# Attention's prologue in a four-stage image kernel: key copies issued from ScalarE's queue, and the first phase's row maxima taken over both PSUM banks at once

## What is computed

```python
qkv = einsum('oc,bct->bot', qkv_w, xf) + qkv_b            # 256 -> 768, t = 1024
scores = einsum('bthe,bThe->bhtT', q, k) / sqrt(32)
attn = softmax(scores, axis=-1)
out = einsum('bhtT,bThe->bthe', attn, v)
```

## Time and profile before

| | us |
|---|---|
| median of 3 runs | 5492.75 (5491.58 to 5498.53) |
| the profiled execution, its own time | 5495.14 |
| its span | 5493.3 |
| granted TensorE clock, mean | 0.853 |
| PE / DVE / ACT / POOL busy | 77% / 66% / 39% / 37% |
| 16 attentions, each with a prologue of some 38 us from the first head to the transposed maxima | about 610 |

### The profile page before, as it was taken

The page is one execution under the profiler, slowest core; times in us unless marked ns, Lnnn a source line. Parts: engine busy times, 40 slices in busy tenths (PEclk is TensorE's granted clock), DMA queues, the critical chain, the costliest instruction groups (busy, mean ns, idle before and its releaser), DMA issues.

```text
span 5493.3 us, 44457 instructions
## 1 busy us (share of the span) xinstructions
PE 4249.1 (77%) x16298; PEld 1843.1 (34%) x16298; DVE 3607.0 (66%) x4793; ACT 2146.6 (39%) x2639; POOL 2007.6 (37%) x681
## 2 busy tenths in 40 slices
PE   5688866879668896688866878669796697866978
PEld 2243422434224332243322433224332243322333
DVE  6763677637776368764687646867468674686746
ACT  3233452334423354243542425424254242542524
POOL 3531435404344043440444504434044340443404
PEclk7689977999769997799977999779897798977999
DMA  0020100210002100022000120011200112001020
GB/s 36 0 55 19 29 8 7 48 29 19 8 8 47 34 14 8 9 47 44 3 8 14 41 46 1 8 25 30 46 1 8 31 24 46 1 8 29 19 46 9
DMA packets 62956, 125.75 MB, mean 23 GB/s; under 512 B 18825, under 2 KB 21001, under 8 KB 62482
## 3 DMA queue, kind: packets, MB, share of 16 engines
q1 hardware_dynamic: 62738, 122.91, 9.6%
HBM read 12.23 MB, written 8.39 MB: 4 GB/s over the span
## 4 chain that ended last, share of the span: by engine, by line
PE 47%; DVE 28%; issue 10%; ACT 7%; SPq 4%; POOL 2%; DMA 2%; DVEq 0%; ACTq 0%; POOLq 0%
DVE mx L954 9%; PE PS L1250 8%; PE PS L1292 8%; PE PS L1087 7%; PE PS L1340 7%; PE PS L1374 4%; DVE work L846 3%; DVE work L848 3%; PE PS L1146 3%; PE PS L1184 2%; ACT PT L624 2%; SPq L290 2%; PE PS L1301 2%; SPq L299 2%; POOL work L392 1%
## 5 line engine op out<-in xcount | busy, mean ns | idle before, releaser
L954 DVE TENSOR_REDUCE mx<-PS 128x1 f32<-128x512 f32 x2048 | 1338.1, 687 | 422.0 <-PE PS L1250 417.9
L624 ACT ACTIVATE PT<-PS 128x1024 f32<-128x1024 f32 x1024 | 1006.9, 1023 | 689.9 <-PE PS L1340 660.0
L1250 PE MATMUL PS<-KS,QS 96*128 96x512 f32 x2048 | 894.9, 479 | 195.4 <-DMA KS<-piece 84.7
L408 POOL TENSOR_TENSOR piece<-PT 128x2048 f32<-128x2048 f32 x48 | 220.0, 4584 | 2183.4 <-ACT PT L624 2183.4
L408 POOL TENSOR_TENSOR piece<-piece,PT 128x2048 f32<-128x2048 f32 x192 | 878.0, 4573 | 58.4 <-ACT PT L624 47.1
L388 POOL TENSOR_TENSOR work<-work,Crep 128x1024 f32<-128x1024 f32 x256 | 616.3, 2409 | 390.5 <-DVE work L846 193.1
L1340 PE MATMUL PS<-QS,KS 98*128 98x512 f32 x2048 | 681.4, 424 | 45.9 <-DMA QS<-nm 22.2
L1250 PEld LDWEIGHTS PS<-KS,QS 96*128 96x128 f32 x2048 | 378.0, 197 | 816.2 <-DVE mx L954 578.0
L1292 PE MATMUL PS<-PT,Vt 128*32 128x512 f32 x4096 | 546.0, 605 | 27.0 <-ACT PT L624 27.0
L1184 PE MATMUL PS<-dstk,sel 128*128 128x512 f32 (+1 forms) x640 | 315.7, 568 | 321.1 <-DVE work L848 133.0
L542 ACT ACTIVATE PS<-PS,Aneg 128x1024 f32<-128x1024 f32 x256 | 278.3, 1087 | 628.5 <-PE PS L1184 597.8
(11 more groups left out here) (198 smaller groups left out, 4983.0 us busy)
## 6 DMA issues: line engine op xcount, KB each, us to landing
QS<-piece SPq DMA_DIRECT2D x384, 128.0 KB, 2.4
KS<-piece SPq DMA_DIRECT2D x384, 128.0 KB, 2.4
xin<-x SPq DMA_DIRECT2D x8, 1024.0 KB
out<-xr SPq DMA_DIRECT2D x8, 1024.0 KB, 4.0
W<-wpack SPq DMA_DIRECT2D x2, 1024.0 KB
QS<-nm SPq DMA_DIRECT2D x128, 8.0 KB, 1.9
W<-wpack SPq DMA_DIRECT2D x1, 576.0 KB
W<-wpack SPq DMA_DIRECT2D x2, 256.0 KB
```

What stands on the lines that cost most here:

```text
L408: pool.tensor_tensor(total, first, PT[:, i % 3, :, :], ALU.add).then_inc(sum_pool.sem, 1)
L624: act.activation(PT[:, i % 3, 2 * pr:2 * pr + 2, :], PS[:, 2 + 2 * pr:4 + 2 * pr, :], ACT.Exp, scale=SCALE).then_inc(p_sb.sem, 1)
L954: dve.tensor_reduce(mx[:, at, cc:cc + 1], PS[:, row_slot(n, cc), :], AX.X, ALU.max).then_inc(r_max.sem, 1)
L1250: pe.matmul(PS[:, row_slot(n, cc), :], QS[0:kd, c, h, q * P:q * P + P], KS[0:kd, h, cc * N:cc * N + N], start=True, stop=True).then_inc(r_ ...
```

## The change

Three edits, all in the prologue of the 16 attentions:

1. The 12 key copies of a group are issued by ScalarE instead of SP, after ScalarE has written both heads of the group and waited for the keys' rest. SP issues the 12 query copies in one go.
2. In phase 0 a row's maximum is one reduction over both halves (1024 scores, two banks), straight into `mboth`. It releases both halves at once (`r_max` rises by two). The joining reduction L961 is gone in phase 0, as is its semaphore step: the transpose waits for the last row's `r_max`.
3. The semaphore `m_both` counts one phase less, and the joining reduction waits in every phase where it is left for the transpose before it.

```diff
@@ sync engine
                     sp.wait_ge(*qk_rest(b, n + 1))
-                    for j in range(AHEAD):
+                    for j in range(GH):
                         queries(j)
-                    sp.wait_ge(*qk_rest(b, n + 2))
-                    for j in range(GH):
-                        for blk, part in enumerate((0, 0, 1)):
-                            sp.dma_start(KS[...], piece[32 * j:32 * j + 32, 1, part, :]).then_inc(stackedk[g][j].sem, 16)
-                        if j + AHEAD < GH:
-                            queries(j + AHEAD)
@@ ScalarE, attention, behind both heads of a group
+                    act.wait_ge(*qk_rest(b, 4 * a + 2 * g + 2))
+                    for j in range(GH):
+                        for blk, part in enumerate((0, 0, 1)):
+                            act.dma_start(KS[...], piece[32 * j:32 * j + 32, 1, part, :]).then_inc(stackedk[g][j].sem, 16)
@@ VectorE, phase 0
                 for n in range(PHASE_ROWS):
-                    for cc in range(NC):
-                        row_max(n, cc)
+                    dve.wait_ge(*r_ps(b, halves(a, n, NC - 1) + 1))
+                    dve.tensor_reduce(mboth[:, n:n + 1], PS[:, row_slot(n, 0):row_slot(n, 0) + NC, :].rearrange("p a n -> p (a n)"),
+                                      AX.X, ALU.max).then_inc(r_max.sem, NC)
@@ TensorE, turn_max
-                    pe.wait_ge(*m_both(b, a * PHASES + ph + 1))
+                    if ph == 0:
+                        pe.wait_ge(*r_max(b, halves(a, PHASE_ROWS - 1, NC - 1) + 1))
+                    else:
+                        pe.wait_ge(*m_both(b, a * (PHASES - 1) + ph))
```

More of the change, by code:

```diff
@@ L53 @@
 TURN_AT = 7
-AHEAD = 3
 NORM_AT = 4
@@ L241, in build @@
         r_ps, r_max = sig("r_ps", 2 * HEADS * KT * NC), sig("r_max", 2 * HEADS * KT * NC)
-        m_both = sig("m_both", 2 * PHASES)
+        m_both = sig("m_both", 2 * (PHASES - 1))
         mt_ps, nm_head, nm_rest = (sig(n, 2 * PHASES) for n in ("mt_ps", "nm_head", "nm_rest"))
@@ L293, in attention @@
                     sp.wait_ge(*qk_rest(b, n + 1))
-                    for j in range(AHEAD):
+                    for j in range(GH):
                         queries(j)
-                    sp.wait_ge(*qk_rest(b, n + 2))
-                    for j in range(GH):
-                        for blk, part in enumerate((0, 0, 1)):
-                            sp.dma_start(KS[32 * blk:32 * blk + 32, GH * g + j, :].bitcast(F32),
-                                         piece[32 * j:32 * j + 32, 1, part, :].bitcast(F32)).then_inc(stackedk[g][j].sem, 16)
-                        if j + AHEAD < GH:
-                            queries(j + AHEAD)
                 for ph in range(PHASES):
@@ L589, in attention @@
                                        bias=v(bq, 2 * kind + g)).then_inc(qk_head.sem, 1)
+                    act.wait_ge(*qk_rest(b, 4 * a + 2 * g + 2))
+                    for j in range(GH):
+                        for blk, part in enumerate((0, 0, 1)):
+                            act.dma_start(KS[32 * blk:32 * blk + 32, GH * g + j, :].bitcast(F32),
+                                          piece[32 * j:32 * j + 32, 1, part, :].bitcast(F32)).then_inc(stackedk[g][j].sem, 16)
                 for q in range(2):
@@ L958, in row_max @@
                         dve.wait_ge(*r_max(b, halves(a, n, NC - 1) + 1))
-                        if ph > 0:
-                            dve.wait_ge(*mt_ps(b, PHASES * a + ph))
+                        dve.wait_ge(*mt_ps(b, PHASES * a + ph))
                         dve.tensor_reduce(mboth[:, :], mx[:, :, :], AX.X, ALU.max).then_inc(m_both.sem, 1)
```

## The result

| | before | with the change |
|---|---|---|
| median of 17 executions each, us | 5493.05 (5489.31 to 5499.03) | 5506.96 (5500.40 to 5518.02) |
| ratio of the times | | 1.0024, 95% interval 1.0017 to 1.0031 |
| the profiled execution, its own time / its span | 5495.14 / 5493.3 | 5505.12 / 5503.4 |
| granted TensorE clock, mean | 0.853 | 0.854 |

The kernel became slower by 0.24%, 13.9 us, where 5467 and a gain of 26 us had been forecast, and it ended just above the range (5503). In the kernel with the change L580 is the line of the heads (L588 before), L943 of the rests (L946), L978 the wide reduction, L951 the 512-wide one of the later phases (L954), L1247 the rows' products (L1250), L1231 the projection of V (L1234), L289 SP's query copies and L585 ScalarE's key copies.

A forecast was written before the change was run, and what follows sets the result against it. No engine bounds the whole; in each of 16 prologues the maxima wait for the last query. From T0 to the transpose -1.3, T0 itself -0.3, times 16 gives -26 us: 5467 by the median, range 5445 to 5503.

The forecast's parts named there:

- What bounds the prologue: In each prologue, the last query's landing, not the first key's, starts VectorE's maxima; ScalarE idles 9.54 us in the mean.
- T0: Start of row 0's maximum on VectorE, 305.98 in the first prologue; forecast to come 0.3 us earlier.
- Two streams carry 1.4 times as much: While queries and keys copy together, the DMA engines carry 1.4 times one stream; the last query lands at 303.0.
- rival B: DMA engines are the bound, or ScalarE issues slowly: T0 +1.7 or +1.3, kernel 0 to +6 us, some 5496; chance 0.25.
- ScalarE's issue as dear as SP's: ScalarE's 12 key issues ahead of the third head take 0.647 us each, as on SP, ending at 303.06.
- Rows 0 to 2, -1.10: `rest(1,1)` starts at T0 + 3.39 instead of T0 + 4.49, if the keys have landed: 1.10 us saved per prologue.
- The 13 rows, no change: Rows 3 to 15 take 15.6 us against 15.63; rows meeting V's projection eat what the wide form saves.
- The join, -0.22: Dropping the joining reduction after the last row saves 0.22 us per prologue; only the hand-over stays.
- C: Keys starve the queries: T0 +4.9, kernel +57 us, 5550; its sign, third head later than 305.0; chance 0.12.
- D: More gain: ScalarE issues at 0.465 us, queries land at 302, T0 -1.5, kernel -45 us, 5448; chance 0.10.
- E: The wide form does nothing, a wide row taking 1.196 us: +8 us on the forecast, 5475; no chance of its own.
- part one: The stretch from T0 to the transpose, 21.60 us before; forecast 1.3 us shorter per prologue.

The follow-up runs named there:

- copies_only: Kernel before with only the key copies moved to ScalarE's queue, maxima 512 wide and joined as before; 5505.44 us against 5494.11, ratio 1.0025.
- short_keys: Changed kernel with group 0's 12 key copies cut to a quarter of their columns in second attentions; transpose there at 37.29 us, 38.63 in first attentions.
- same_half: Changed kernel with SP's queries in head order 2, 3, 0, 1, so both streams read the same half; 5520.97 us in a single execution.
- spread_wide: Kernel before with wide maxima, rows 0 and 1 before `rest(1,0)`, `rest(1,1)` behind row 5, V spread further among rows; 5457.35 us, ratio 0.9922.
- v_early: Kernel before with wide maxima, V projected ahead of row 0, rows 0 and 1 before `rest(1,0)`, `rest(1,1)` behind row 5; 5487.00 us, ratio 0.9998.

## Why the prediction was wrong, by its own steps

**What bounds the prologue: right.** The last query, not the first key, starts the maxima. When it landed later, T0 moved with it: +1.86 and +1.87 with the change, +1.86 for T0 in `copies_only`.

**Two streams carry 1.4 times as much: wrong, and this is the step that failed.** The prediction called it its weakest. It read 400 GB/s of a load to all 128 partitions, against 207 of a copy between blocks of 32, as room that a second stream could use. The windows of the first prologue show 1.14 and 1.05 times, the 16 prologues 1.12. The prediction's own sum for engines that carry no more than now has the last query land at 305.3, T0 at +1.7. That is rival B, and nearly what came (+1.87). `short_keys` shows the mechanism (the bytes of the keys), `same_half` that the idea of halves was no error, only worth some 10% instead of 40%. B's sum came so near partly by luck. At 1.12 times the rate it would give 297.3 + 8.0 / 1.12 = 304.4 and T0 at +0.8. What it lacks is a delay where the streams join: in the medians the sixth query lands at 8.23 us, the seventh at 10.63, the next five every 1.03. In the kernel before, the seventh comes 0.60 behind the sixth. What holds it up no run shows. The 93 to 95% busy share under one stream, which the prediction lists as B's evidence, was the row to go by. The rule that it cites beside B (all issuers' DMAs interleave on the same engines; the Trainium skill, "DMA: Bandwidth & Descriptors", "Issuing engines are not separate DMA queues") comes near these windows, which show 1.12 times and not 1.4.

**ScalarE's issue as dear as SP's: nearly right.** 8.80 / 12 = 0.73 us an issue where 0.647 was assumed, 0.67 when the engines have less to carry. It didn't bind: ScalarE was through 1.1 us before the last query landed.

**Rows 0 to 2, -1.10: right.** `rest(1,1)` starts at T0 + 3.39 to the digit (310.47 - 307.08), and the first row behind it at T0 + 4.58 against 4.59 forecast. The keys had landed by then, 0.78 earlier than before.

**The 13 rows, no change: a little off.** 15.8 to 15.9 instead of 15.6, the 0.2 us that is missing from the -1.3. I can say where it went only for the forms: in `copies_only` the 26 halves take 15.62, so here the wide form costs 0.2 to 0.3 where the keys are early. Three wide rows in a run start every (3.48 - 1.22) / 2 = 1.13 us, as forecast; a long run does not keep that, ten rows of `spread_wide` at a clock of 1.00 start every 1.18.

**The join, -0.22: right**, and the only place at which the wide form won by itself. In all it is worth 0.13 to 0.18 a prologue, some 2 to 3 us of the kernel, where 0.2 + 0.22 had been booked to it. In `v_early` it lost 0.74 a prologue, 12 us.

**The sum.** Forecast (-1.3 - 0.3) x 16 = -26. Measured -1.13 + 1.87 = +0.74, 11.8 us by the medians. The table of stretches gives +6.7 for the prologues, since two of them were 2.7 to 3 us longer than the rest in the profiled execution of before; +4.5 each for phases and the stretches between; and -5.6 ahead of the first and behind the last. As those stretches move by as much between kernels that don't differ there, the last 2 of the 13.9 us have no cause that I could show.

**The rivals.** C (keys starve the queries) had a landing of +4.9; it came at +1.86, so C was not it, although its sign did come: the third head moved by +1.87, to 305.5 on the prediction's scale, beyond 305.0. That sign could not tell C from B, whose own sum gives 305.3. D fell with the 1.4. E, the wide form that does nothing, was nearly true as well. B's net of +0.4 lay 0.34 short of what came, half of it in T0 (1.87 for 1.7), half in part one (-1.13 for -1.3), and 16 x 0.34 = 5 us, with the 2 that have no cause, took the result out of "the same". I had given B no share of slower, though its 6 us lay near the edge of 11.

## What to carry to other kernels

A copy that an engine issues early doesn't come free when another stream already keeps the DMA engines over 90% busy: it delays that stream, so ask first which of the two is waited for. Here the waited-for stream was delayed by 1.9 us to have the other one 0.8 us sooner. The better use of such a wait is work that needs neither stream: with two rows of maxima taken ahead of the rest that hangs on the last query, V spread over the rows and `rest(1,1)` behind row 5, the transpose came 1.65 us earlier (36.42 for 38.07), with the copies untouched. T0 itself moved by 3 us, so half of what an early start wins can go again in the waits behind it.

Before work is moved away from TensorE's stretches to relieve them, look at the granted clock of the stretch that it leaves; and measure a wide form at the clock at which it will run, since it gains little while the producer is ahead and loses when it isn't.

## What the runs showed of the hardware that I had not expected

- Two streams that read the same half of the partitions carried no more than one: 205 GB/s against 202 from 9 to 16 us behind the first head, and a pair of copies in 1.3 us, as one stream needs for two. With different halves it was 226.
- An issue takes longer when the engines are full. ScalarE's twelve took 8.08 us with a quarter of the bytes, 8.80 with full ones, 11.50 in `same_half`, so an engine that issues DMAs ahead of its own work is held up by them.
- TensorE's granted clock stood at 0.50 while it was busy 4.4 to 5.0 of 5.0 us with rows alone, and at 1.00 with V's products between the rows. A row's two products take 1.19 us at the one level and 0.82 at the other. `v_early` and `spread_wide` differ only in V's place, copies and banks, and the transpose came 1.17 us earlier in the second.
- The stretches between attentions, with the same code, differ by up to 4 us each with the granted clock. Over 15 of them that came to 19 us between two kernels, as much as a whole us saved in every prologue.
